# A fused vision tower on one core: matrix products in f32 instead of split f16, and scatter rows loaded by SP

## The reference, cut to what matters

```python
q  = _ln(reduce_feats, ln_q_w, ln_q_b) @ Wq.T          # one query for each 4x4 window
kv = _ln(unf, ln_kv_w, ln_kv_b) @ Wkv.T                # keys, values of its 16 pixels
h  = reduce_feats + softmax(q * scale @ k) @ v @ proj_w.T + proj_b
h  = concatenate([cls_tok, h], axis=1)                 # 32 x 257 x 256

xp = _layernorm(h) @ W_ih.T + b_ih + b_hh              # recurrence: the image is the time step
step: h_new = tanh(xp_t + h_prev @ W_hh.T)
h  = h + hiddens

tok = _layernorm(h); probs = softmax(tok @ router_w.T); top 2, weights renormalised
out = tok + sum over the two experts: w_e * (gelu(tok @ w1[e] + b1[e]) @ w2[e] + b2[e])
h   = h + out
```

## Time and profile before

| what | us |
|---|---|
| median of 3 runs (1470.38 to 1484.2) | 1472.1 |
| the profiled execution: first to last instruction | 1542.8 |
| PE busy | 1342.3 (87%) |
| DVE busy | 1067.5 (69%) |
| ACT busy | 832.4 (54%) |
| POOL busy | 711.1 (46%) |

### The profile page before, as it was taken

How to read it: one execution, slowest core, us unless ns; L and a number is a source line. 1 busy time by engine, 2 the same in 40 slices (tenths; PEclk the granted TensorE clock), 3 DMA queues, 4 the chain that set the end, 5 groups by cost and what they waited for, 6 DMA issues and landing times. The chain is left out here.

```text
span 1542.8 us, 63164 instructions
## 1 busy us (share of the span) xinstructions
PE 1342.3 (87%) x25681; PEld 1061.8 (69%) x25681; DVE 1067.5 (69%) x2855; ACT 832.4 (54%) x2065; POOL 711.1 (46%) x854
## 2 busy tenths in 40 slices
PE   4899999999999999999999999999959997688670
PEld 3677777777777777777776776677748896467550
DVE  4677777777777777878666666678756764467464
ACT  1455665655655655555555555555647774355340
POOL 2243343444434434343555555553313777552555
PEclk9999999999999999999999999999989998799795
DMA  7998898988998998988888989897245887687677
GB/s 259 407 307 298 293 308 297 305 295 295 310 297 276 314 293 280 294 278 293 303 309 302 300 306 312 296 313 256 71 153 193 272 283 245 186 267 255 207 232 227
DMA packets 186620, 423.78 MB, mean 275 GB/s; under 512 B 23968, under 2 KB 89312, under 8 KB 186208
## 3 DMA queue, kind: packets, MB, share of 16 engines
q1 hardware_dynamic: 170336, 380.27, 73.2%
q0 software_dynamic: 14048, 38.16, 7.8%
q10 hardware_dynamic: 1952, 1.32, 0.3%
HBM read 332.26 MB, written 87.39 MB: 272 GB/s over the span
## 5 line engine op out<-in xcount | busy, mean ns | idle before, releaser
L1146 DVE BATCH_NORM_STATS2 st<-xp 128x6 f32<-128x512 f32 x512 | 339.8, 695 | 16.4 <-DMA xp<-xpix 16.0
L656 POOL TENSOR_TENSOR rs_px<-px_ve,half_neg 128x16 f32<-128x16 f32 x64 | 187.0, 2922 | 179.9 <-DVE px_ve L1151 179.9
L770 ACT ACTIVATE zT<-bank 128x512 f32<-128x512 f32 x256 | 138.7, 597 | 75.3 <-PE bank L983 75.2
L1465 POOL DMA_INDIRECT y<-ys_dram,slot x130 | 126.3, 971 | 112.5 <-DVE fin L1628 47.1
L641 POOL TENSOR_TENSOR q_rs<-q_ve,half_neg 128x1 f32<-128x1 f32 x64 | 35.1, 549 | 289.7 <-DVE q_ve L1163 289.7
L763 ACT ACTIVATE z_s<-bank 128x512 f32<-128x512 f32 x256 | 138.6, 597 | 49.0 <-PE bank L973 49.0
L942 PE MATMUL bank<-xc,u 128*32 128x64 f32 x8192 | 149.4, 220 | 17.6 <-issue 17.0
L942 PEld LDWEIGHTS bank<-xc,u 128*32 128x32 f32 x8192 | 132.1, 110 | 41.3 <-issue 32.2
L893 PE MATMUL bank<-xp,spread 128*32 128x256 f32 x2048 | 140.4, 390 | 19.7 <-DMA xp<-xpix 13.4
L744 ACT ACTIVATE u<-bank 128x512 f32<-128x512 f32 x256 | 132.2, 602 | 41.5 <-PE bank L921 41.4
L983 PE MATMUL bank<-ident,z_s 128*128 128x128 f32 x1024 | 150.3, 279 | 1.9 <-issue 1.0
(11 more groups left out here) (195 smaller groups left out, 3398.5 us busy)
## 6 DMA issues: line engine op xcount, KB each, us to landing
xp<-xpix SPq DMA_DIRECT2D x256, 512.0 KB
xc<-xg SPq DMA_DIRECT2D x256, 512.0 KB
xc<-xs_dram SPq DMA_DIRECT2D x86, 256.0 KB
ys_dram<-y_s SPq DMA_DIRECT2D x86, 256.0 KB
xs_dram<-zero SPq DMA_DIRECT2D x57, 384.0 KB
base_dram<-h SPq DMA_DIRECT2D x65, 128.0 KB
rows_dram<-tok SPq DMA_DIRECT2D x65, 128.0 KB
hb<-base_dram SPq DMA_DIRECT2D x65, 128.0 KB
```

Of the source, the lines that this page charges most:

```text
L656: pool.tensor_tensor(rs_px[:, :], px_ve[:, :], half_neg[:, :], ALU.pow).then_inc(s["px_done"], 1)
L770: act.activation(zT[:, c, :, :].rearrange("p h (a r t) -> p r h a t", r=2, t=TS)[:, r, :, :, :], BIG[f][:, :].rearrange("p (a h t) -> p h ...
L1146: dve.bn_stats(st[:, j, :], xp[u.x][:, 2 * j:2 * j + 2, :].rearrange("p i c -> p c i")).then_inc(s["st_done"], 1)
L1465: pool.indirect_dma_start(y[q][0:n, :], None, ys_dram[g], bass.IndirectOffsetOnAxis(ap=slot_u[k][0:n, t:t + 1], axis=0)).then_inc(ga_in[q] ...
```

## The change

In the recurrence and in both expert layers the split halves go; the operands stay f32 and each product is one f32 matmul call: 8 calls a unit instead of 24, 8 calls of 256 columns a tile instead of 24. With them go ACT's and DVE's splitting steps, the scale `WSC`, and the splits of `W_ih`, `W_hh`, `w1` and `w2`. `w1` and `w2` are loaded one slot earlier (62 and 63), straight into `xp0` and `xp1`. The first layer's weights are no longer addressed by PE through the table: DVE reads the expert and copies its weights into one of three buffers (`w1_now`, 128x512 f32, three tiles ahead). In a slot's order ACT does `q_out` ahead of `exps`, PE does `turn_tok` ahead of `turn_p` and `logits` ahead of `turn_h`. In the second stage SP loads all 34 blocks left to scatter, each into a buffer of its own, in batches of up to four; POOL only scatters, and takes the normalisation of block 64 after the first six blocks. The plan's spacing goes from 0.82 to 1.05 steps.

```diff
@@ recurrence (PE)
                 for c in range(CC):
-                    mm(o, hh_h[:, c, w], hT_h[z.two][:, c, 0:n], start=(c == 0), stop=False)
-                    mm(o, hh_h[:, c, w], hT_l[z.two][:, c, 0:n], start=False, stop=False)
-                    mm(o, hh_l[:, c, w], hT_h[z.two][:, c, 0:n], start=False, stop=False)
+                    mm(o, hh_s[:, c, w], hT[z.two][:, c, 0:n], start=(c == 0), stop=False)
                 for c in range(CC):
-                    mm(o, ih_h[:, c, w], xnT_h[:, c, 0:n], start=False, stop=False)
-                    mm(o, ih_l[:, c, w], xnT_h[:, c, 0:n], start=False, stop=False)
-                    last = mm(o, ih_h[:, c, w], xnT_l[:, c, 0:n], start=False, stop=(c == CC - 1))
+                    last = mm(o, ih_s[:, c, w], xnT[:, c, 0:n], start=False, stop=(c == CC - 1))
@@ slot, PE
+                if late:
+                    turn_tok(pe, u.k - 4, FB)
                 if mid:
                     turn_p(pe, v)
-                if late:
-                    turn_tok(pe, u.k - 4, FB)
...
+                if late:
+                    logits(pe, u.k - 4, FB)
                 if end:
                     turn_h(pe, z)
-                if late:
-                    logits(pe, u.k - 4, FB)
@@ slot, ACT
+                if front:
+                    q_out(act, u)
                 if mid:
                     exps(act, v)
-                if front:
-                    q_out(act, u)
...
-                if end:
-                    hidden_high(act, z)
...
-                for k in weights_now(u.k):
-                    weights_high(act, k)
@@ slot, DVE
-                if end:
-                    token_low(dve, z)
...
-                    hidden_low(dve, z)
...
-                for k in weights_now(u.k):
-                    weights_low(dve, k)
@@ SP, first stage
-            sp.wait_ge(s["rec_w"], 3)
...
+                if u.k == UNITS - 2:
+                    sp.wait_ge(s["z_ps"], 2 * (UNITS - 3))
+                    for e in range(E):
+                        sp.dma_start(w1_s[:, e, :, :], w1[e].rearrange("(c p) n -> p c n", p=P)).then_inc(w1_in, 16)
@@ second stage, plan and SP
-            ready.append(max(ready[-1] + 0.82, BEFORE[group_of(t)] + TILES[group_of(t)] + 3.5))
+            ready.append(max(ready[-1] + 1.05, BEFORE[group_of(t)] + TILES[group_of(t)] + 3.5))
...
+            def load_rows(sp, i):
+                row_ready(sp, ROWS[i][-1])
+                for t in ROWS[i]:
+                    sp.dma_start(xrow2[t - SIZES[0]][:, :], rows_dram[t]).then_inc(rows_in[i], 16)
...
+            for i in range(len(ROWS)):
+                if group_of(ROWS[i][0]) == 1:
+                    load_rows(sp, i)
...
+                if 9 <= k < 9 + len(ROWS) and group_of(ROWS[k - 9][0]) == 2:
+                    load_rows(sp, k - 9)
@@ second stage, POOL
-            for t in rest[:RX2 - 1]:
-                load_row(pool, t, *ring)
-            for t in rest:
-                scatter(pool, t, *ring)
-                if t + RX2 - 1 in rest:
-                    load_row(pool, t + RX2 - 1, *ring)
+            for t in rest[:6]:
+                scatter_late(pool, t)
+            route_scale(pool, UNITS)
+            route_base(pool, UNITS)
+            for t in rest[6:]:
+                scatter_late(pool, t)
@@ second stage, PE and DVE
-                        mm(o, wh, xh, start=(c == 0), stop=False)
-                        mm(o, wh, xl, start=False, stop=False)
-                        last = mm(o, wl, xh, start=False, stop=(c == CC - 1))
+                        last = mm(o, w1_now[k % 3][:, c, m * P:(m + 1) * P], xT[k % 3][:, c, :], start=(c == 0), stop=(c == CC - 1))
...
-                        mm(o, h, wh, start=(m == 0), stop=False)
-                        mm(o, h, wl, start=False, stop=False)
-                        last = mm(o, l, wh, start=False, stop=(m == CC - 1))
+                        last = mm(o, gl[k % 3][:, m, i * P:(i + 1) * P], w, start=(m == 0), stop=(m == CC - 1))
...
+                dve.tensor_copy(w1_now[k % 3][:, :, :], w1_s[:, bass.ds(e, 1), :, :].rearrange("p e c n -> p (e c) n")).then_inc(s["w1_set"], 1)
...
-                if 0 <= k + 1 < N:
-                    halves(dve, k + 1)
-                if 0 <= k + 4 < N:
-                    low(dve, k + 4)
+                if 0 <= k + 3 < N:
+                    chosen[k + 3] = weights_of(dve, k + 3)
```

More of the change, by code:

```diff
@@ L28 @@
 XPARTS = 4
-WSC = 64.0
 EPS = 1e-5
@@ L228, in vit_tower @@
         xn = sa("xn", [P, C])
-        xnT_h, xnT_l = [sa(f"xnT_{n}", [P, CC, P + 1], F16) for n in "hl"]
-        hT = sa("hT", [P, CC, P + 1])
-        hT_h = [sa(f"hT_h{i}", [P, CC, P + 1], F16) for i in range(2)]
-        hT_l = [sa(f"hT_l{i}", [P, CC, P + 1], F16) for i in range(2)]
+        xnT = sa("xnT", [P, CC, P + 1])
+        hT = [sa(f"hT{i}", [P, CC, P + 1]) for i in range(2)]
         zero = sa("zero", [P, C])
@@ L404, in load_row, with scatter @@
             sp.dma_start(xrow[i][:, :], rows_dram[t]).then_inc(xrow_in[i], 16)
[L406 removed]
+        def scatter(pool, t):
             g = group_of(t)
[L409 removed]
+            i, q = t % RX, t // RX
             n = B if t == UNITS else P
@@ L1036, in turn_h @@
                 for c in range(CC):
-                    last = pe.transpose(RB[:, c * P:(c + 1) * P], hT[:, c, 0:P], ident[:, :])
+                    last = pe.transpose(RB[:, c * P:(c + 1) * P], hT[z.two][:, c, 0:P], ident[:, :])
                 last.then_inc(s["ht_ps"], 1)
@@ L1230, in token_norm @@
                                   ALU.mult).then_inc(s["xn_done"], 1)
-            def token_low(dve, z):
-                wait(dve, s["xnT_done"], z, 1, 1)
-                dve.tensor_tensor(xnT_l[:, :, 0:P], RB[:, 0:C].rearrange("p (c t) -> p c t", t=P), xnT_h[:, :, 0:P],
-                                  ALU.subtract).then_inc(s["xnl_done"], 1)
-            def hidden_low(dve, z):
-                n = P + 1 if z.two == 0 else P
-                wait(dve, s["hh_done"], z, 1, 1)
-                dve.tensor_tensor(hT_l[z.two][:, :, 0:n], hT[:, :, 0:n], hT_h[z.two][:, :, 0:n],
-                                  ALU.subtract).then_inc(s["hl_done"], 1)
             def token_out(dve, z):
@@ L1405, in load_x @@
                 if j == 0 and g > 0:
-                    for q in range(RX2):
-                        sp.wait_ge(sent2[q], 32 * len(range(q, FIRST[g] + SIZES[g] - SIZES[0], RX2)))
+                    sp.wait_ge(sent2[g - 1], 32 * SIZES[g])
                 if k >= XT:
```

191 lines of the change are left out of this document (72 added, 119 removed).

## The result

The kernel after has a median of 1495.7 us in 4 runs (1494.1 to 1497.6), beside 1471.8 for the kernel before: a ratio of 1.0149, 95% interval 1.0103 to 1.0194. It is slower by 1.5%, 23.9 us, where 48.5 were forecast: the sign was right, the size was half of the forecast. Medians and ranges are of all runs; a ratio leaves out runs over 1.5% above the fastest of the same kernel.

A forecast was written before the change was run, and what follows sets the result against it. PE was taken to set the pace in both stages, with some 30 us of stalls in the timed runs. Second stage +66 and first -17.5 gave +48.5 on 1472.1: 1520.6 us; own range 1498 to 1545, wider range 1474 to 1563.

The forecast's parts named there:

- The tile of 4.41: Second stage, PE: upper bound of a tile in us, with f32 passes of 0.248; 3.92 was forecast.
- rival (2): First stage: reordering covers nothing, ACT's queue being later; +0.46 a slot instead of -0.11, +35 us, 1555; chance 0.07.
- the wait for `qT` goes, -0.16: First stage, each slot: `q_out` ahead of `exps` removes PE's wait ahead of `project`, 0.16 us a slot.
- The recurrence's section: First stage, PE from recurrence start to `weigh`: 3.37 us becomes 3.42, +0.05; without the reordering 0.46 longer.
- Start and drain: Both ends of the first stage: PE's waits for weight splitting shrink, -2.5 us at the start, -8 in the drain.
- the stage before "without stalls", 322 us: Second stage of the kernel before, from PE's start, counted without stalls; the trace has 389.6 us.
- 1306 + 25 x 3.05 = 1382, tile 85's at 1437: Second stage before, behind tile 42: results follow at PE's undisturbed 3.05 us a tile, tile 67's at 1382.
- (3): Stalls with POOL's indirect DMA bursts go; 1454 us, decides from more than 48.5 us of stalls saved; chance 0.11.
- (4): Stalls left in the timed runs go, and a little more, 34 to 48 us: 1473 to 1487; chance 0.09.
- Rival (1): Second stage: 46 scatters back to back cost PE up to 1 us each, +14 to +46: 1535 to 1567; chance 0.15.
- the forecast's signs: Recurrence 16 matmuls at 0.114 us, those waits gone, slot 16.1 to 16.2, tiles 3.9 apart, POOL idle before gathers, 22 late blocks.
- the signs of being wrong: Tile at most 3.1 us, slot over 16.6, PE standing during early second-stage scatters, or POOL setting the end from its first gather.

The follow-up runs named there:

- the second profile: The kernel before, unchanged, profiled again; 1472.1 us in 8 runs, ratio 0.999; this profiled execution took 1481.35 us.
- POOL's ring in its place: The kernel after, but POOL loads its scatter rows itself into a ring of four, as before, instead of SP; 1492.4 us, ratio 1.012 to the kernel before.
- one of them: The kernel before with only the change's first stage: f32 recurrence, reordered slot, no split of its weights at the start; 1447.9 us, ratio 0.983.

## Why the prediction was wrong, point by point

**A matmul in f32: right as a number, not as a reason.** 0.112 us a pass at 128 columns (0.114 forecast), 0.216 at 256 (0.217), a tile of 3.89 us (3.92). The tile of 4.41 is out, and so is rival (2), an uncovered +0.46: even without the new order a slot is 16.23 us. But I read 0.114 as twice the f16 time, that is as columns; 64 columns take as long.

**First stage: the step that failed is "the wait for `qT` goes, -0.16".** The 0.16 is an average over 34 slots of which 22 show the wait. The slot of the earlier trace rows is one of the others: its 16.29 us have no such wait, but a stop on the scores' line:

```profile
612.75 0.24 PE L942 MATMUL bank<-xc,u 128*32 128x64 f32 x1 [0.37 <-issue]
```

Where PE is late for one reason it does not wait for the other. In an undisturbed slot the wait is the whole 0.35 us (16.23 to 15.88). The recurrence's section came out as forecast (+0.05; measured 3.37 and 3.37), though by another way: f32 takes the place of a wait of 0.41 that I had read as 0.20, and that without the new order. The forecast's own numbers say nearly as much: `turn_h` at 606.76 instead of 606.70 makes the section 0.06 longer without the new order, not 0.46. So it is -0.34 a slot (16.22 to 15.88) for -0.11, and over the 63 slots -20.1 for -7, which is 13 us of the miss. Start and drain are 3.6 us better than their -10.5.

**Second stage: the step that failed is the stage before "without stalls", 322 us, and in it the count behind tile 42, "1306 + 25 x 3.05 = 1382, tile 85's at 1437".** It takes PE alone to set the pace there. The loop over tiles was counted as 269.8 us and is 286.4 in the second profile (281.4 to 288.0 in four more with the same second stage). Up to tile 42 the count is right, with the wait for the late gathers in it: 138.8, measured 138.1. Behind it 131 were counted and 148.3 measured. There DVE has finals in its list, planned 0.82 steps apart, so that in eight steps it has two, and these steps are 4.70 us long. In the kernel after DVE makes no low halves, at 1.05 no step has two finals, and nearly every step is PE's 3.89. So 17 us that the forecast took for PE's 3.05 a tile were in the timed kernel, went with the change, and were not in the sum. Some 3 of them were gathers still late; the rest goes, as far as the steps can tell, with DVE's list, and where the gathers come in time PE waits 8.8 us for DVE. The cause that rivals (3) and (4) spoke of, stalls that go, was at work, but for 16.6 us: short of the 34 from which (4) decides, and of the 48.5 of (3). The time of 1495.7 lies between (4) and the forecast's own range from 1498.

**What I did not price.** The normalisation of block 64 behind twelve scatters costs 7 us (it is in the diff, named in the text ahead of the prediction, and has no term). In the tail 32 gathers are left behind the last result and not 28, 5 us, and POOL waits 4 us for rows that SP loads late: +10 where +3 was reckoned. The loop of the kernel after is 334.6 for 333 only because faster tiles and the short last four make up for the 7.

**The sum.** 48.5 - 13 (slots) - 3.6 (start and drain) - 15 (the loop: 48.2 for 63) + 7 (tail) = 23.9. That the tail hides 7 us of the other misses is luck.

**Signs and rivals.** Rival (1), a burst that stops PE, is out: PE was busy 143.0 of 143 us from 1153 on, and POOL's ring in its place changed nothing on PE but the one step. In the trace the forecast's signs came true (tile, 16 passes at 0.112, no wait ahead of `turn_h` or for qT, POOL idle, 22 late blocks) but for the slot of 16.1 to 16.2. One of the signs of being wrong came true as well: PE stood still while POOL scattered in the first 80 us of the second stage, 4.50 us ahead of block 64's tokens, though from the order of POOL's list and not from the burst. The base was at fault: the profile ahead of the prediction was 70.7 us longer than the timed runs, I counted every stop as a chance one, and though by that count 30 us of stops were left in the timed runs, I added a difference without stops to their median.

## What to carry to other kernels

Read a wait from start to start, in slots that nothing else disturbs, before multiplying it; an average over all slots hides that two delays cover each other. Before a stall is written off as contention, look at what stands in the waiting engine's list: an in-order engine that finishes old work (a `final`) ahead of new work passes the lateness of a slow queue on to everybody, and a step into which a plan puts two pieces of such work is longer than one with one. So reckon a stage step by step for each engine's list, not at the pace of the busiest engine. When a step moves in a list, price the step itself as well as what it was moved for; here twelve scatters ahead of one tiny instruction cost what SP's loads brought. And try the halves of a change alone: one of them was 1.7% faster by itself.

## What the runs showed of the hardware that was not expected

A pass of an f32 matmul with 128x128 weights starts 0.112 us after the one before whether it has 43, 64 or 129 columns (0.111 with the 8 of `logits`), and 0.216 with 256; the weight load beside it is given as 192 ns, that of an f16 pass in the kernel before as 98. Splitting the columns of such a product in two doubles its time: +102 us for the kernel. The Trainium skill (TensorE: Matmul & The Clock Gate, "Weight-path perf modes") excludes f32 from the fast weight load; that a floor of 0.112 comes from the load would fit it, but no run here tells the load from another fixed cost.

PE stands still now and then until a 16 KB block of code has come, which the page lists among the DMA queues. At a DMA share of 0.89 it did so for 29 us in 660 on one line of short matmuls, at 0.58 for 0.6 us. In the 14 profiles with all pixels every stop without another cause over 0.2 us from 60 to 720 us, 6 to 29 in each, ended 1.1 to 1.7 us behind the end of such a block.
